# Two attention blocks and a feed-forward on one core: the reciprocals of the row sums turned by the DMA instead of TensorE

## The reference

```python
qh = (q @ w_q).reshape(B, L, N_HEAD, D_K).transpose(0, 2, 1, 3)      # kh, vh alike from the context
attn = jnp.einsum('bhqd,bhkd->bhqk', qh * scale, kh) + add_attn
attn = jnp.where(mask == 0, NEG_INF, attn)
attn = jax.nn.softmax(attn, axis=-1)
out = jnp.einsum('bhqk,bhkd->bhqd', attn, vh)
out = out.transpose(0, 2, 1, 3).reshape(B, L, N_HEAD * D_V)
out = out @ w_o + residual                                            # then layer norm
...
x = _ln(x + _mha(x, x, sa_..., mask), ln1_g, ln1_b)
x = _ln(x + _mha(x, memory, ca_..., None), ln2_g, ln2_b)
h = jax.nn.relu(_linear(x, ff_w1, ff_b1))
x = _ln(x + _linear(h, ff_w2, ff_b2), ln3_g, ln3_b)
```

## Time and profile before

| | us |
|---|---|
| median of 3 runs (3896.86 to 3903.61) | 3898.04 |
| the profiled execution | 3891.58 |
| its span | 3889.8 |
| PE busy in it | 3737.0 (96%) |
| DVE busy | 2753.3 (71%) |
| ACT busy | 2234.0 (57%) |
| POOL busy | 1866.1 (48%) |

### The profile page before, as it was taken

The page is one execution under the profiler, slowest core; times in us unless marked ns, Lnnn a source line. Parts: engine busy times, 40 slices in busy tenths (PEclk is TensorE's granted clock), DMA queues, the critical chain, the costliest instruction groups (busy, mean ns, idle before and its releaser), DMA issues.

```text
span 3889.8 us, 63432 instructions
## 1 busy us (share of the span) xinstructions
PE 3737.0 (96%) x20588; PEld 2778.0 (71%) x20588; DVE 2753.3 (71%) x5817; ACT 2234.0 (57%) x4852; POOL 1866.1 (48%) x1917
## 2 busy tenths in 40 slices
PE   8999999999999998999999999999999989999999
PEld 6776777777777766776676766666766758888887
DVE  6666666577777777888888887888888863444434
ACT  6555555555555556878878777777777752111111
POOL 4434443333443435777777656666666632112101
PEclk9999999999999999999999999999999999999999
DMA  7667767554555566666666647666666683122200
GB/s 202 191 189 200 199 195 203 134 151 126 138 139 133 136 183 175 169 169 169 169 171 167 149 145 197 174 171 165 156 167 166 171 219 95 60 66 72 67 29 33
DMA packets 867944, 584.64 MB, mean 150 GB/s; under 512 B 641825, under 2 KB 690977, under 8 KB 866593
## 3 DMA queue, kind: packets, MB, share of 16 engines
q1 hardware_dynamic: 853648, 538.63, 52.2%
q10 hardware_dynamic: 13968, 41.95, 3.3%
HBM read 189.29 MB, written 237.50 MB: 110 GB/s over the span
## 4 chain that ended last, share of the span: by engine, by line
PE 39%; ACT 6%; DVE 6%; issue 6%; POOL 5%; DMA 1%; SPq 1%; DVEq 0%; POOLq 0%; ACTq 0%
PE psV L1594 5%; POOL QS L2431 4%; PE psT L1563 4%; PE psS L1542 3%; PE psS L1487 3%; PE psS L1489 3%; PE psS L1488 3%; PE psJ L1487 3%; PE psJ L1488 2%; PE psJ L1489 2%; PE psT L1487 2%; PE psT L1489 2%; PE psT L1488 2%; ACT PR L1874 2%; DVE PR L2079 2%
## 5 line engine op out<-in xcount | busy, mean ns | idle before, releaser
L2431 POOL TENSOR_SCALAR QS<-QK 32x1024 fp32r<-32x1024 f32 (+2 forms) x1152 | 1232.0, 1069 | 838.1 <-DVE QK L2093 409.3
L1874 ACT ACTIVATE PR<-PR,MN 128x512 f32<-128x512 f32 x1536 | 1101.6, 718 | 607.8 <-DVE MN L2075 458.0
L2075 DVE CUSTOM_DVE_ANT_0 PR<-psS,RAW 128x512 f32<-128x512 f32 x1024 | 693.9, 682 | 393.8 <-PE psS L1539 306.0
L1563 PE MATMUL psT<-ID,PR 128*128 128x128 f32 x3912 | 595.8, 275 | 60.1 <-ACT PR L1874 56.0
L1563 PEld LDWEIGHTS psT<-ID,PR 128*128 128x128 f32 x3912 | 472.5, 141 | 191.7 <-ACT PR L1874 98.4
L1594 PE MATMUL psV<-plain 128*32 128x512 f32 (+1 forms) x3072 | 507.0, 608 | 15.0 <-DMA plain<-split_rows 6.1
L1542 PE MATMUL psS<-QS 128*128 128x512 f32 x1024 | 451.9, 443 | 26.8 <-DVE PR L2079 12.4
L2079 DVE TENSOR_SCALAR_CACHE_REDUCE PR<-psS 128x512 f32<-128x512 f32 x512 | 344.4, 682 | 102.9 <-PE psS L1542 100.6
L1913 ACT ACTIVATE PR<-psS,COLS 128x512 f32<-128x512 f32 x128 | 88.3, 690 | 565.8 <-PE psS L1489 565.7
L2171 DVE COPY plain<-psT 128x512 f32<-128x512 f32 x530 | 361.5, 682 | 0.0
L2145 DVE CAST QK<-PR 128x512 fp32r<-128x512 f32 x128 | 64.7, 505 | 354.3 <-ACT PR L1913 318.1
(11 more groups left out here) (161 smaller groups left out, 8351.6 us busy)
## 6 DMA issues: line engine op xcount, KB each, us to landing
split_rows<-plain SPq DMA_DIRECT2D x366, 256.0 KB, 2.8
split_rows<-RAW SPq DMA_DIRECT2D x192, 256.0 KB, 2.6
x<-Y SPq DMA_DIRECT2D x96, 256.0 KB, 2.4
RAW<-x SPq DMA_DIRECT2D x96, 256.0 KB, 3.8
Y<-x SPq DMA_DIRECT2D x96, 256.0 KB, 3.4
kept_c<-R SPq DMA_DIRECT2D x32, 512.0 KB, 4.1
kept<-ROWS SPq DMA_DIRECT2D x32, 512.0 KB, 3.8
R<-kept_c ACTq DMA_DIRECT2D x8, 2048.0 KB, 8.9
```

What stands on the lines that cost most here:

```text
L1563: mm = nc.tensor.transpose(dst[:, kt * P:(kt + 1) * P], prob(st, k)[:, kt * P:(kt + 1) * P], ID[:, :])
L1874: nc.scalar.activation(prob(st, k), prob(st, k), ACT.Exp, bias=MN[:, k % 8:k % 8 + 1], scale=-1.0, accum_out=row_sums(st, SM, g)[:, qt, j: ...
L2075: nc.vector.tensor_tensor_reduce(out=prob(st, k), in0=psS[:, n % 2], in1=FB[:, k % NT], scale=-st.scale, scalar=BIG, op0=ALU.add, op1=ALU. ...
L2431: nc.gpsimd.tensor_scalar(to, pair, 1.0, 1.0, ALU.mult, ALU.mult).then_inc(stacked, 1)
```

## The change

R_TURN goes. SPREAD now writes RB as 16-bit halves, and two new steps of SP, R_BOUNCE and R_FETCH, send RB to DRAM and bring it back into RB itself through the DMA transpose. SCALE waits for that and reads RB instead of psT. RECIP, SPREAD and the two new steps get slots: in L0 RECIP 6.5 (from 8), SPREAD 7.5 (from 9.5), R_BOUNCE 8.5, R_FETCH 9.75; in SA and CA RECIP 5 and SPREAD 6 as before, R_BOUNCE 7, R_FETCH 9; SCALE is at 12 everywhere, as before. The tiles beside RB are now steps 9 and 25 in L0 and 11 in SA and CA. In L0 the split of step 0 of each group is done by POOL, not DVE. In the last batch of L0a the loads of the weight blocks K and V of L0b get later slots, and two of their splits (V 1 and V 3) slots of their own.

```diff
+SPLIT_BY_POOL = {64:(0,),32:()}
...
-    "RECIP": 8,
-    "SPREAD": 9.5,
-    "R_TURN": 10.5,
-    "PASS": 11,
+    "RECIP": 6.5,
+    "SPREAD": 7.5,
+    "R_BOUNCE": 8.5,
+    "R_FETCH": 9.75,
     "SCALE": 12,
...
     "RECIP": 5,
     "SPREAD": 6,
-    "R_TURN": 10.25,
-    "PASS": 11,
+    "R_BOUNCE": 7,
+    "R_FETCH": 9,
     "SCALE": 12,
...
-        ('J_LO', ('K', 2), 'L0a', 0): 13, ('W_LOAD', (('L0b', 'K', 0), 0), None, 0): 13,
+        ('J_LO', ('K', 2), 'L0a', 0): 13, ('W_LOAD', (('L0b', 'K', 0), 0), None, 0): 15.6,
...
         def beside(st):
 
-            return (7, 15) if st.dk == 64 else (7,)
+            return (9, 25) if st.dk == 64 else (11,)
...
+            def bounce_reciprocals():
+
+                i = reciprocals[0]
+                reciprocals[0] += 1
+                sp.wait_ge(r_spread, i + 1)
+                if i >= 2:
+                    sp.wait_ge(r_fetched, 16 * (i - 1))
+                sp.dma_start(r_rows[i % 2], RB.bitcast(U16).rearrange("p (h k) -> p h k", h=2)).then_inc(r_bounced, 16)
+
+            def fetch_reciprocals():
+
+                i = reciprocals[1]
+                reciprocals[1] += 1
+                sp.wait_ge(r_bounced, 16 * (i + 1))
+                sp.dma_start_transpose(RB.rearrange("p (t q) -> p t q", t=NT).bitcast(U16),
+                                       r_rows[i % 2].rearrange("q h k -> (q h) k")).then_inc(r_fetched, 16)
...
-            def turn_reciprocals(st, g, b):
-                i = tal["spread"].next()
-                pe.wait_ge(r_spread, tal["spread"].done(i))
-                dst = turn_place(st, b, ("R", g))
-                for tt in range(NT):
-                    mm = nc.tensor.transpose(dst[:, tt * P:(tt + 1) * P], RB[:, tt * P:(tt + 1) * P], ID[:, :])
-                mm.then_inc(t_full, 1)
...
             def largest(st, k, first, b):
 
                 n = tal["s"].next()
                 before = tile_before(st, b, k)
+                if k in beside(st) and scaled[0]:
+                    dve.wait_ge(o_scaled, scaled[0])
...
             def scale_group(st, g, b):
-                dve.wait_ge(t_full, turned_at[st.name, b, ("R", g)])
+                n = scaled_at[st.name, b, g]
+                scaled[0] = n
+                dve.wait_ge(r_fetched, 16 * n)
                 dve.wait_ge(pv_evac, tal["pv_own"].done(tal["pv_own"].n - 1))
-                nc.vector.tensor_tensor(OG[:, :], turned((st.name, b, ("R", g))), OG[:, :], ALU.mult).then_inc(t_evac, 1)
+                nc.vector.tensor_tensor(OG[:, :], RB, OG[:, :], ALU.mult).then_inc(o_scaled, 1)
...
+            def split_prob(st, k, b):
+                tile = st.name, b, k
+                n = sent_at[tile]
+                settle(False)
+                pool.wait_ge(exp_done, exp_at[tile])
+                if n >= 4:
+                    pool.wait_ge(bounced[n % 4], times(n - 4))
+                issued("split")
+                nc.gpsimd.tensor_scalar(halves(tile), prob(st, k).bitcast(U16).rearrange("p (k h) -> p h k", h=2), 1.0, 1.0,
+                                        ALU.mult, ALU.mult).then_inc(p_split_pool, 1)
+
...
-                wide = row_sums(st, RS, g).unsqueeze(3).to_broadcast([P, NT, st.per_group, st.dk])
-                nc.gpsimd.tensor_scalar(RB[:, :].rearrange("p (t j d) -> p t j d", t=NT, j=st.per_group), wide,
+                n = st.per_group * NT
+                wide = RS[:, g % 2, 0:n].bitcast(U16).rearrange("p (n h) -> p h n", h=2).unsqueeze(3).to_broadcast([P, 2, n, st.dk])
+                nc.gpsimd.tensor_scalar(RB.bitcast(U16).rearrange("p (h n d) -> p h n d", h=2, d=st.dk), wide,
                                         1.0, 1.0, ALU.mult, ALU.mult).then_inc(r_spread, 1)
```

More of the change, by code:

```diff
@@ L61 @@
     "P_HI",
-    "PASS",
     "SPLIT",
@@ L91 @@
     "TURN",
-    "R_TURN",
+    "R_BOUNCE", "R_FETCH",
     "UP", "RELU", "HIDDEN", "DOWN", "SUMS",
@@ L414, in timetable @@
         if last:
-            for step in ("RECIP", "SPREAD", "R_TURN", "PASS", "SCALE", "GROUP_HI", "GROUP_LO"):
+            for step in ("RECIP", "SPREAD", "R_BOUNCE", "R_FETCH", "SCALE", "GROUP_HI", "GROUP_LO"):
                 after = table[step]
@@ L479, in last_batch @@
         late |= {("GATHER", 3): DRAIN_PV[3] + 0.5}
-        late |= {("RECIP", 3): 33, ("SPREAD", 3): 34, ("GROUP_HI", 3): 41.5, ("GROUP_LO", 3): 41.5}
+        late |= {("RECIP", 3): 33, ("SPREAD", 3): 34, ("R_BOUNCE", 3): 35, ("R_FETCH", 3): 36.5, ("GROUP_HI", 3): 41.5, ("GROUP_LO", 3): 41.5}
         return [(late.get((step, what), slot) if slot >= st.steps else slot, step, what) for slot, step, what in own]
@@ L1085, in split_by_act, with split_by_pool @@
         def split_by_act(st, k):
-            return k % (st.per_group * NT) in SPLIT_BY_ACT[st.dk]
+            return k % (st.per_group * NT) in SPLIT_BY_ACT[st.dk] and not split_by_pool(st, k)
+        def split_by_pool(st, k):
+            return k % (st.per_group * NT) in SPLIT_BY_POOL[st.dk]
         def value_part(name):
@@ L1120, in count_turns @@
                     orders[step].append((st.name, b, k))
-                if step in ("TURN", "R_TURN"):
-                    turned_at[st.name, b, k if step == "TURN" else ("R", k)] = len(turned_at) + 1
-                elif step == "SCALE" or step == "P_LO" and not by_act(st, k):
+                if step == "TURN":
+                    turned_at[st.name, b, k] = len(turned_at) + 1
+                elif step == "SCALE":
+                    scaled_at[st.name, b, k] = len(scaled_at) + 1
+                elif step == "P_LO" and not by_act(st, k):
                     done[t_evac] += 1
-                    evacuated[st.name, b, k if step == "P_LO" else ("R", k)] = t_evac, done[t_evac]
+                    evacuated[st.name, b, k] = t_evac, done[t_evac]
                 elif step == "P_HI" and by_act(st, k):
@@ L1166, in tile_before @@
             if k in beside(st):
-                return (st.name, b, ("R", 0)) if k == 15 else (last.name, (i - 1) % B, ("R", NG - 1)) if i else None
+                return None
             mine, others = ([n for n in range(s.steps) if n not in beside(s)] for s in (st, last))
@@ L1385, in run @@
                     b = data(st, batch + off if at is None else at)
-                    if step == "MAX":
+                    if step == "R_BOUNCE":
+                        bounce_reciprocals()
+                    elif step == "R_FETCH":
+                        fetch_reciprocals()
+                    elif step == "MAX":
                         tal["s"].next()
@@ L1906, in centre, with relu @@
                                      scale=RD[:, tt:tt + 1]).then_inc(y_centred, 1)
-            def relu(f):
+            def relu(f, first=False):
+                if first and f == 3:
+                    act.wait_ge(o_scaled, len(scaled_at))
                 n = tal["u"].next()
@@ L2212, in run @@
                         prob_lo(st, k, batch + off if at is None else at)
-                    elif step == "SPLIT" and not split_by_act(st, k):
+                    elif step == "SPLIT" and not split_by_act(st, k) and not split_by_pool(st, k):
                         split_prob(st, k, batch + off if at is None else at)
@@ L2322, in settle @@
                 sems = dict(spread=r_spread, pieces=stacked, res=res_ready, rstd=rstd, shifted=y_shifted,
-                            laid_lo=laid_lo, weights=w_rest, tile=tile_lo, planes=f_planes)
+                            laid_lo=laid_lo, weights=w_rest, tile=tile_lo, split=p_split_pool, planes=f_planes)
                 if last_op[0] and (shifts or last_op[0] == "pieces"):
@@ L2489, in run @@
                         beside_turn[0] = turned_at[st.name, batch + off if at is None else at, k]
+                    elif step == "SPLIT" and split_by_pool(st, k):
+                        split_prob(st, k, batch + off if at is None else at)
                     elif step == "SPREAD":
-                        spread(st, k)
+                        spread(st, k, batch + off if at is None else at)
                     elif step == "RES":
```

26 lines of the change are left out of this document (17 added, 9 removed), and 26 rows, old and new, of the table SEAM.

## The result

The change made the kernel slower. Before 3898.1 us and after 3993.9 us (medians of five runs each, 3896.9 to 3903.6 and 3990.3 to 4000.9); the ratio is 1.0242, 95% interval [1.0231, 1.0253], 96 us. The forecast was 3858 us, with 3894 as the end of its range. The profiled execution took 3990.29 us, its span 3988.5 us.

A forecast was written before the change was run, and what follows sets the result against it. PE was taken as the bound, with the loop through DVE and ACT close behind in SA and CA. Turns give -52.5 us, a third of DVE's 35 costs 12, net -40: 3898.0 - 40 = 3858 us, range 3828 to 3894.

The forecast's parts named there:

- the time that the round trip takes: From the start of SPREAD: spread 1.10, out 2.6, back 3.5, sum 7.2 us; 5.8 at best, 11.3 at worst.
- SCALE from two SBUF inputs: SCALE on DVE takes 0.30 us more beside POOL: 19 us in SA and CA, 19 in L0.
- longer spread: SPREAD on POOL takes 1.10 us instead of 0.65, 29 us more in L0, and adds to SCALE's slowing.
- transfers and SP's order, nobody waiting: 128 transfers each way: landings longer by tenths; in group 3 tile 0's bounce 3.4 us late but covered.
- The price of a turn: PE is freed of 0.41 us for each of 128 R_TURNs, 52.5 us, half in L0; bounds 0 and 81.
- 81 us gone from PE's busy time: Sign that the forecast holds: no transposes of RB on PE, and their 81 us missing from its busy time.
- Covered in L0, with 4 us to spare: In L0, 4.5 slots or 12.5 us from SPREAD to SCALE, against 7.2 to 8 us for the path.
- Late only in group 3, by 0.8 to 1.2 us: DVE waits at SCALE 1.2 us in SA, 0.8 in CA, together 16 us; groups 0 to 2 in time.
- A third of 35 us reaches PE: In SA and CA DVE gets 16 + 19 = 35 us more, of which 12 us reach PE.
- The split on POOL: In L0, 64 splits move: DVE loses 54 us, POOL gains 71; counted as nothing, 0 to about 7 won.
- the seam: Eight weight loads in L0a's last batch go 1 to 4 slots later: cost 0, at worst 2 to 3 us.
- The rival that ended slower: In-order SP and long landings make four groups a batch late in SA and CA: 3926 us, chance 0.13.

The follow-up runs named there:

- q_base: The kernel before with every transposing transfer replaced by two plain copies of the same bytes, values not the reference's: 3882.9 us, ratio 0.995, one timing.
- q_changed: The changed kernel with all its transposing transfers, R_FETCH too, replaced by two plain copies each: 3960.5 us, ratio 1.0162.
- q_one_turn: q_base with one transpose in each R_TURN instead of four, all waits and DVE work kept: 3849.8 us, ratio 0.988.
- q_scale_sbuf: q_base with its turns kept, but SCALE multiplies by a constant unit matrix in SBUF instead of the turned tile in PSUM: 3918.6 us, ratio 1.0051.
- q_later_sa_ca: q_changed with SCALE and the two group parts in later slots in SA and CA only, L0 unchanged: 3922.1 us, ratio 1.0061.
- q_scale_later: q_changed with SCALE and the two group parts in later slots in SA, CA and L0: 3953.5 us, ratio 1.0139.

## Why the prediction was wrong

Two steps failed. The first is the time that the round trip takes against the time that it has: 7.2 us "covered" in L0 and in groups 0 to 2, 16 us of waiting in all, where DVE waited 118 us. The second is the third of DVE's added time that was to reach PE, where about two thirds did. The account, from q_base to q_changed, and beside each the prediction's term (each of the first four rows is one experiment beside another, and the first two carry q_base's 10 us):

| | measured | predicted |
|---|---|---|
| turns off PE (four thirds of q_one_turn) | -44 | -52.5 |
| SCALE from two SBUF inputs | +36 | a third of 19: +6 |
| longer spread | +7 | with the row above |
| split on POOL (L0) | +2 | 0 |
| rest, within the error of q_base | +4 | 0 (seam) |
| transfers and SP's order, nobody waiting | +11 | 0 |
| the wait at SCALE | +61 | a third of 16: +5 |
| sum | +78 | -40 |
| transposes in place of copies | +18 | |

- **The price of a turn** held: 0.41 us from the starts in the earlier trace rows against 0.34 (33 us for 96 of the 128 turns' worth), not the 0.63 of busy time. For the same reason the sign "81 us gone from PE's busy time" was set too high; 50 us would have gone without the clock. The clock itself had no term in the sum, and it took 56 us.
- **Covered in L0, with 4 us to spare** failed. In SA and CA the path from the start of the spread to the landing took 7.3 us in the median, as forecast. In L0 it took 12.9, against the 12.5 of the slots, and DVE waited 55 us there. The 7.2 us were a sum of medians of SA, as if SP were free at each step. In L0 the way out is issued 2.2 us behind the start of the spread and takes 3.3 us to land; then 2.9 us pass before SP issues the way back, which takes 3.7 (medians). The way back stands behind transfers of SP that wait for something else. At 164.22 the reciprocals left in L0a, and at 168.50 they had landed; their way back was issued at 172.26:

```profile
164.22 0.38 SPq L1368 DMA_DIRECT2D r_rows<-PR  x1
164.69 0.56 SPq L1357 DMA_DIRECT2D split_rows<-plain  x1
165.31 0.62 SPq L1342 DMA_DIRECT2D half<-Y  x1
169.83 0.33 SPq L1241 DMA_DIRECT2D Y<-in_ctx_t  x1
170.21 0.43 SPq L1342 DMA_DIRECT2D half<-Y  x1
170.74 1.48 SPq L1384 DMA_TRANSPOSE plain<-split_rows  x1
172.26 1.73 SPq L1375 DMA_TRANSPOSE PR<-r_rows  x1
```

  The row was also read wrongly: it says `issue`, and the spread at 1013.65 came 0.15 us behind the end of the reciprocal that had begun at 1013.3. POOL had waited for that, not for tile 15.
- **Late only in group 3, by 0.8 to 1.2 us** came out for SA in the sum (9.4 us in 8 batches; 9.6 forecast), and that was luck: the single waits are 0 to 3.4 us with a median of 0.6, and group 1 waits 5.3 us in the first batch. In CA group 3 waits 12.3 us in the last batch and 2.5 in the other seven together. It was wrong above all for group 2 of CA, which meets a load of 2 MB on another queue. The margins were read group by group for SA and only for group 3 in CA. The load stood in the table at the very slot of R_BOUNCE, 51.5 against 51.
- **A third of 35 us reaches PE** failed too, in both factors. The 35 us left out L0's half of SCALE, and q_scale_sbuf lost 12 of its 39 us of span in L0. Of the 118 us of waiting, 94 lay where I had reckoned none. In the copied pair the 92.7 us of waiting cost 61 us, two thirds; of SCALE's and the splits' 61 us, 36 arrived, six tenths. The small waits of PE in the earlier trace rows did not mean that the loop had room; and the longer gaps of PE brought half speed with them.
- **The split on POOL** and **the seam** counted 0; the first was 2 us, which is no difference, the second was not tried by itself.
- The rival that ended slower named the right mechanism, the queue and the landings, and put it at 3926: it had the price and the place wrong (four groups of SA and CA a little late, none in L0), and its factor of a third was the same mistake. By the rule of the Trainium skill, GPSIMD Engine Reference, section Specifications, DVE instructions with two SBUF inputs contend with POOL. The traces agree: in q_scale_sbuf SCALE goes from 0.68 to 1.06 us with the second input moved from PSUM to SBUF, and in the changed kernel it takes 0.68 to 0.69 us wherever POOL does nothing beside it. So the term of 0.30 us was a price of POOL's company, 0.27 us in the changed kernel, and of the right size.

## What to carry to other kernels

A round trip through DRAM costs more than its two transfers, here 12.9 us in L0 in place of 7.2: ask what each queue can be holding when each half has to be issued, over every group and batch, and what large transfer shares the slot. Before an operand is moved from PSUM to SBUF, price the instruction that reads it, beside what the other engines do at the same time; here it took back 36 us of the 44 that TensorE won in the form with the constant, an estimated 21 with the reciprocals, and reading the other operand from PSUM gave it back. Small waits of the fullest engine do not show that an engine close behind it has room: of what was added to DVE, two thirds arrived here and not a third. That share is of this kernel and these two experiments; q_later_sa_ca took 42 us of waiting away and won 38, q_scale_later took 69 away and won 7.

## What was not expected of the hardware

- The same product of 512 fp32 elements takes DVE 0.68 us with one input in PSUM. With both in SBUF it takes 0.68 to 0.69 us where POOL is idle beside it and up to 1.72 us where it is not, 0.96 to 1.09 us in the mean of a run.
- A gap of PE of 2.45 us was followed by stretches at a granted clock of 0.72 and 0.62, with starts of 512-column matmuls 0.43 us apart instead of 0.23.
- A 2 MB load on ACT's queue stretched a 256 KB transfer on SP's queue from 2.6 to 8.5 us, with the DMA engines at 0.84 of their time.
- With two plain copies in pieces of 256 bytes for each transposing transfer the whole kernel took 3882.9 us against 3902.0, each timed once: the transposing form cost 0.5%.
